# A gated-delta-rule block on one core: where the inverse's read-back waits, and where the merge steps stand among the projections

## The reference

```python
q = short_conv(hidden_states @ Wq, conv_wq).reshape(b, t, NUM_HEADS, HEAD_K)
k = short_conv(hidden_states @ Wk, conv_wk).reshape(b, t, NUM_HEADS, HEAD_K)
v = short_conv(hidden_states @ Wv, conv_wv).reshape(b, t, NUM_HEADS, HEAD_V)
beta = jax.nn.sigmoid(hidden_states @ Wb)
g = -jnp.exp(A_log) * jax.nn.softplus(hidden_states @ Wa + dt_bias)
o = gated_delta_rule(q, k, v, g, beta)
gate = (hidden_states @ Wg).reshape(b, t, NUM_HEADS, HEAD_V)
...
def _step(S, xs):
    qt, kt, vt, gt, bt = xs
    S = S * jnp.exp(gt)[..., None, None]
    pred = jnp.einsum('bhk,bhkv->bhv', kt, S)
    delta = (vt - pred) * bt[..., None]
    S = S + jnp.einsum('bhk,bhv->bhkv', kt, delta)
    return (S, jnp.einsum('bhk,bhkv->bhv', qt, S))
```

## Time and profile before

| | us |
|---|---|
| median of 3 runs | 1102.63 (1102.19 to 1105.66) |
| the profiled execution, its own time | 1100.91 |
| its span, first to last instruction | 1099.1 |
| TensorE busy, matmuls | 1044.1 (95%) |
| VectorE busy | 627.4 (57%) |
| ScalarE busy | 377.8 (34%) |
| GpSimd busy | 212.1 (19%) |

### The profile page before, as it was taken

How to read it: one execution, slowest core, us unless ns; L and a number is a source line. 1 busy time by engine, 2 the same in 40 slices (tenths; PEclk the granted TensorE clock), 3 DMA queues, 4 the chain that set the end, 5 groups by cost and what they waited for, 6 DMA issues and landing times.

```text
span 1099.1 us, 18622 instructions
## 1 busy us (share of the span) xinstructions
PE 1044.1 (95%) x7356; PEld 843.5 (77%) x7356; DVE 627.4 (57%) x986; ACT 377.8 (34%) x691; POOL 212.1 (19%) x166
## 2 busy tenths in 40 slices
PE   3899999999888999999989999999999999999998
PEld 2686667777677888888777787888888888888886
DVE  3778354999884677787766333333333433434356
ACT  3567465354445333333455112121121212122110
POOL 0332100011014545544331000000000000004191
PEclk8899999999899999999999999999999999999999
DMA  6503336736629465666622000010010100001223
GB/s 199 181 30 115 71 65 164 220 97 185 104 60 225 94 144 131 160 163 143 209 74 77 1 1 30 29 34 25 1 58 1 58 1 30 29 1 67 77 77 115
DMA packets 153399, 97.35 MB, mean 89 GB/s; under 512 B 93536, under 2 KB 130656, under 8 KB 153184
## 3 DMA queue, kind: packets, MB, share of 16 engines
q1 hardware_dynamic: 153312, 96.16, 32.0%
HBM read 64.67 MB, written 31.46 MB: 87 GB/s over the span
## 4 chain that ended last, share of the span: by engine, by line
PE 76%; DVE 12%; issue 4%; ACT 3%; DMA 2%; SPq 2%; POOL 0%; DVEq 0%; ACTq 0%
PE ps L1206 72%; DVE t L1795 5%; DVE t L1887 3%; ACT t L1523 3%; PE ps L1214 3%; DVE t L1800 1%; PE ps L1406 1%; DMA t<-in_x 1%; SPq L1086 1%; DMA t<-scrA 1%; SPq L1143 1%; DVE t L1875 1%; DMA t<-scrU 0%; DVE t L1805 0%; DVE t L1987 0%
## 5 line engine op out<-in xcount | busy, mean ns | idle before, releaser
L1206 PE MATMUL ps<-t,t 128*128 128x512 f32 (+6 forms) x6488 | 990.3, 337 | 37.2 <-DMA t<-in_wmod 8.6
L1206 PEld LDWEIGHTS ps<-t,t 128*128 128x128 f32 (+4 forms) x6488 | 785.3, 166 | 218.5 <-issue 38.8
L1795 DVE TENSOR_TENSOR t<-ps,t 128x512 f32<-128x512 f32 (+4 forms) x306 | 208.2, 700 | 257.4 <-PE ps L1206 242.9
L1523 ACT ACTIVATE t<-t 128x512 fp32r<-128x512 f32 (+7 forms) x342 | 190.8, 579 | 327.3 <-DVE t L1795 202.3
L1795 DVE TENSOR_TENSOR t<-t,t 128x512 fp32r<-128x512 f32 (+16 forms) x209 | 164.9, 794 | 116.2 <-ACT t L1523 104.4
L1523 ACT ACTIVATE t<-ps 128x512 f32<-128x512 f32 (+5 forms) x202 | 108.9, 551 | 313.7 <-PE ps L1206 304.9
L2265 POOL TENSOR_TENSOR t<-t,t 128x512 f32<-128x512 f32 x16 | 22.2, 1390 | 375.2 <-DVE t L1795 373.1
L1887 DVE SCALAR_TENSOR_TENSOR t<-ps,t,t 128x511 f32<-128x511 f32 (+2 forms) x108 | 80.3, 747 | 9.0 <-ACT t L1523 6.2
L1214 PE MATMUL ps<-t,t 128*128 128x128 f32 (+1 forms) x388 | 56.8, 280 | 12.2 <-DVE t L1800 9.8
L1214 PEld LDWEIGHTS ps<-t,t 128*128 128x128 f32 (+1 forms) x388 | 43.5, 143 | 25.7 <-DVE t L1800 14.5
L1523 ACT ACTIVATE t<-ps,t 128x512 f32<-128x512 f32 (+2 forms) x96 | 56.9, 621 | 17.8 <-PE ps L1214 9.1
(11 more groups left out here) (49 smaller groups left out, 232.4 us busy)
## 6 DMA issues: line engine op xcount, KB each, us to landing
scrU<-t SPq DMA_DIRECT2D x60, 256.0 KB, 3.0
t<-in_wf SPq DMA_DIRECT2D x16, 768.0 KB, 4.1
t<-scrU SPq DMA_DIRECT2D x32, 288.0 KB, 4.8
t<-in_wmod SPq DMA_DIRECT2D x6, 1024.0 KB, 6.8
t<-scrU SPq DMA_DIRECT2D x32, 192.0 KB, 3.5
t<-in_W SPq DMA_DIRECT2D x19, 256.0 KB, 2.9
t<-in_x SPq DMA_DIRECT2D x16, 256.0 KB, 4.3
t<-in_x SPq DMA_DIRECT2D x32, 128.0 KB, 2.8
```

Of the source, the lines that this page charges most:

```text
L1206: return e.matmul(o, l, r_, start=start, stop=stop, skip_group_check=True)
L1523: return e.activation(o, i, f, **kw)
L1795: return e.tensor_tensor(o, a, b, op)
```

## The change

Three edits. (1) The stores of the inverse signal three semaphores, `d_pp0` to `d_pp2`, in place of one. `inv2_back` of slice s waits only for the stores that hold its blocks, 96 s to 96 s + 95; `clear_p` on GpSimd still waits for all three. (2) The pauses behind the read-backs are six in place of three. (3) While the merge runs (`merging`: inverse made, lane 0 running, before tile 14), a projection is emitted in two halves, k = 0, 1 and k = 2, 3; one step of lane 0 stands between them.

```diff
-    def project(h, b, wn):
+    def project(h, b, wn, ks=(0, 1, 2, 3)):
         i = pr["n"] % 4
         pr["n"] += 1
-        step("proj", h=h, b=b, bank=i, wn=wn, free=bank_free.get(i))
+        step("proj", h=h, b=b, bank=i, wn=wn, free=bank_free.get(i), ks=ks)
         return i, tick("proj")
...
-        for _ in range(3):
+        for _ in range(6):
             yield
         made["inverse"] = 1
...
+            merging = n < 14 and made["inverse"] and running[0]
+            ks = (0, 1) if merging else (0, 1, 2, 3)
             if b < 3:
-                ahead.append(project(nxt, b + 1, wn))
+                ahead.append(project(nxt, b + 1, wn, ks))
...
-                ahead.append(project(nxt, 0, wn))
+                ahead.append(project(nxt, 0, wn, ks))
+            second = {**plan[-1], "ks": (2, 3)} if merging else None
...
+            if merging:
+                side(0, 1)
+                plan.append(second)
             for l in (2, 3, 0, 1):
                 side(l)
...
-                    e.dma_start(blocks[128 * i:128 * i + 128], Pp[:, i, :, :]).then_inc(sem("d_pp"), 16)
+                    e.dma_start(blocks[128 * i:128 * i + 128], Pp[:, i, :, :]).then_inc(sem(f"d_pp{i}"), 16)
             elif kind == "inv2_back":
                 s = st["s"]
-                e.wait_ge(sem("d_pp"), 48)
+                for i in (96 * s // 128, (96 * s + 95) // 128):
+                    e.wait_ge(sem(f"d_pp{i}"), 16)
                 e.wait_ge(*at_least(st["cleared"]))
...
-                for k in range(4):
+                for k in st["ks"]:
                     e.wait_ge(sem("p_lo"), 4 * b + k + 1)
                     t = mm3(bank(st["bank"]), WH[h][:, k, :], WL[h][:, k, :], Hhi[:, b, k, :], Hlo[:, b, k, :],
                             k == 0, k == 3)
-                t.then_inc(sem("proj"), 1)
+                if k == 3:
+                    t.then_inc(sem("proj"), 1)
...
                 elif s == 2:
-                    e.wait_ge(sem("d_pp"), 48)
+                    for i in range(3):
+                        e.wait_ge(sem(f"d_pp{i}"), 16)
```

## The result

The changed kernel is slower: 1105.82 us median (1101.51 to 1109.58, 18 runs) against 1101.95 for the kernel before on the same chips, a ratio of 1.0032 (95% interval 1.0023 to 1.0041). The forecast was 1103.6, +1.0 us on its baseline; the measured difference is about +3.5. The time lies inside the forecast's range, but that range took in both rivals and is 10 us wide; the sum's own ends were -1.2 and +3.4, and the difference lies just above the upper one. It comes out at the slower rival's +3.7, not at the likeliest case. One run of e6_after_free took 1493.32 us at a granted clock of 0.66 and stands in no ratio; every other run named here is a fast one.

The account below looks back on a forecast made before the run. TensorE holds 76% of the chain, but VectorE bounds the merging stage. Taps end 2.6 us earlier, yet the first unit's later load lands the last store 1.0 us later: 1102.63 + 1.0 = 1103.6, range 1097.2 to 1107.0.

Parts of the forecast that it names:

- the sum's own ends: Last tap ending at 320.0 or 323.4, with 7.5 or 8.7 us for the final transfers: -1.2 and +3.4 us.
- slower rival: TensorE's low clock lasts until 293.5 or longer (1.0 more) and falls again later (1.7 more): +3.7, 1106.3; chance 0.27.
- Own stores: At the inverse's read-backs: waiting only for their own stores takes off 0.2 us, at most 0.24.
- The start two slots on, and no wait at the first product: Merge starts in slot (7,0) instead of (6,2); TensorE's 3.62 us wait for the read-back goes.
- ScalarE's wait: In slot (7,0), ScalarE stands from 277.9 to 285.3 for a store queued behind 16 read-backs; TensorE idles 7.1 us.
- VectorE as the bound of the stage: Merging stage: VectorE needs 32.4 us from 288.1, plus 1.5 for low clock; taps end at 322.0, 2.6 us gained.
- a sign against itself: VectorE holes between 291 and 322 would mean the merging stage's bound changed and the last tap's forecast end is off.
- The split's credit of 0.35: Merge steps inside projections bring products before VectorE asks, taking 0.35 of at most 0.85 us off the merging stage.
- The give-back: Behind the last tap: seven merge products remain, delaying unit 0's load to 334.0 and the last store to 341.7; +1.0 us.
- second low stretch in the tail: Slower rival's part: the clock falls again between (8,3) and (14,2), where TensorE is the bound; 1.7 us more.
- faster rival: ScalarE doesn't stand at the merge's start; last store lands at 335.4: -5.3 us, 1097.3; chance 0.20.
- The idle rule: At TensorE's first merge product: removing the wait (3.6) and half the low stretch (3.4) would gain 7.0 us.

Follow-up runs that it names:

- e6_after_free: Changed kernel, but the loads of the first two units no longer wait for the end of the merge; 1102.68 us, ratio 0.9997 to the kernel before.
- e1_store: Kernel before with only the first edit, each read-back waiting for its own store; 1102.66 us, ratio 1.0002 to the kernel before.
- e4_spread: Changed kernel with the read-backs issued one slice a slot, stores of tile 6 between them; 1100.17 us, ratio 0.9977 to the kernel before.
- the second execution: Second profiled execution of the changed kernel, itself unchanged; it took 1107.64 us.
- the first execution: First profiled execution of the changed kernel, the slowest of its 18 runs; it took 1109.58 us.
- e7_fill: Changed kernel with 29 unused matmuls ahead of the first B product, to keep TensorE busy; 1106.67 us, ratio 1.0035 to the kernel before.
- e3_split: Kernel before with only the third edit, a merge step in the middle of each projection; 1101.92 us, ratio 0.9995 to the kernel before.
- e2_late: Kernel before with only the second edit, six pauses instead of three, projections whole; 1104.54 us, ratio 1.0026 to the kernel before.
- e5_spread_free: e4_spread, with the loads of the first two units no longer waiting for the merge's end; 1096.35 us, ratio 0.9941 to the kernel before.
- e10_tail: e5_spread_free with the projections of tile 14 split too; 1095.74 us, ratio 0.995 to the kernel before.

## Why the prediction was right, and where its size was off

**Own stores.** Forecast 0.2 us, at most 0.24; 0.12 measured, no difference in time (e1_store). Right.

**The start two slots on, and no wait at the first product.** Right: the chain has no wait for the landing of a read-back, and A(0) ran at 278.

**ScalarE's wait.** Forecast until 285.3, 7.4 us long, with TensorE idle for 7.1: 7.42 and 7.61 us, 6.58 and 6.80 measured. e4_spread removes it by moving nothing but the read-backs' place in SP's queue. This cause is shown.

**VectorE as the bound of the stage.** T, the end of the last tap, was put at 322.0, 51.7 us behind the first read-back of the forecast (270.55 less 0.2); the second execution has 51.7, the first 55.2. The forecast lets VectorE run on from 288.1 and allows 1.5 us for TensorE's low clock. The chain shows another course: behind the stall TensorE is the bound for 15.05 us in the first execution and for 11.28 in the second, then VectorE, and from 322.88 on, 3.8 us ahead of T, TensorE again. In the first execution VectorE has the holes that the forecast named as a sign against itself, 2.57 us ahead of 296.30 (for TensorE) and 2.21 ahead of 303.69 (for ScalarE). With e7_fill, at full clock, the stretch is 50.6, so the low clock costs 1.1 where it is short and 4.6 where it is long. That 51.7 was met to the tenth is partly luck: it holds for the short low stretch alone, and the kernel before and e1_store differ by 2.6 here. The split's credit of 0.35 can't be told from nothing (e3_split).

**The give-back.** The mechanism was right (e6_after_free), and here the sum is short, in two terms. *From the last tap to the load of unit 0* the forecast was 12.0; it is 13.0 in both executions of the changed kernel, in e4 and in e7. The term that was mis-sized is TensorE's place at T: the forecast has A(12), and so projection (14,0) ahead of it, done at T - 0.25. In the first trace GpSimd's fill, which that projection releases, starts 0.52 behind T (326.65), and ScalarE's eviction of A(12) 1.00 behind it:

```profile
327.17 1.38 POOL L2210 MEMSET t<- 128x1536 f32 x1 [52.77 <-PE ps L1213]
...
327.65 0.67 ACT L1531 ACTIVATE t<-ps 32x192 f32<-32x192 f32 x2 [2.97 <-PE ps L1213]
```

In e2_late, whose projections are whole, the fill starts at 321.62, 0.49 ahead of its T (322.11), and the load 12.3 behind T. So the forecast counted the split as a gain for VectorE alone; the half of (14,0) that it puts behind a merge step is 0.7 of the missing 1.0, as far as two traces can tell. *From there to the landing of the last store* it was 7.7; to the load of Wo, 0.1 later, 9.3 and 8.5 were measured, 9.6 and 9.8 in e7 and e4. The term that was mis-sized is the rate: 1.66 MB at the 266 GB/s of one window, plus one us. The landing of the last store behind three other transfers took 4.82 and 4.40 us where the row of before had 3.09, and 5.40 and 5.58 in e7 and e4; the 8.7 that I had set as the upper end is passed in three of the four traces. In the second execution projection (14,3) ended 16.7 us behind T, where 13.7 was forecast, with 3.4 us at half rate from 335.5 on. As SP's queue was busy until 339.58 anyway, this held up the last store by 0.36 only.

Put together for the second execution: T as forecast, 1.0 and 1.6 more behind it, against a forecast of +1.0: 3.6, with 3.7 seen over the stage (73.95 against 70.21) and about +3.5 in the ratio. For the first execution the same sum gives +6.6 over the stage, more than the ratio, so the agreement rests on the choice of the trace.

**The rivals.** The slower one has the right time (+3.7) for a reason that isn't the main one. Its second low stretch in the tail is there in the second trace:

```profile
334.00:338.00 4.00, 3.89 (x34) 3.19 (x35) 1.39 (x4) 0.06 (x1) 0.00 (x0) 0.70 0.33 74
338.00:342.00 4.00, 3.81 (x63) 3.14 (x62) 0.20 (x1) 2.66 (x4) 1.93 (x3) 0.88 1.19 265
```

but in the first trace the clock is 1.00 there and the tail is nearly as long (21.6 and 22.3 us from the last tap to Wo), and e7_fill, with the clock at 1.00 through both stretches, is as slow. Its first part, a low clock beyond 293.5, is there in the first execution and not in the second. So e2_late and e6_after_free put the loss on the later start and the waiting loads, but how much of it the clock carries in a usual run is open. The faster rival (-5.3, no wait of ScalarE) is what e4_spread builds; it came to 0.23% (2.5 us) under the kernel before, since the give-back stands, and to 0.59% (6.5) with the loads freed (e5). The chance of 0.26 for slower and 0.52 for no change was the wrong way round for a loss of 0.32%, right at the edge between them.

**The idle rule.** By the rule of the Trainium skill (TensorE: Matmul & The Clock Gate, "Why this matters for your kernels"), to leave TensorE no idle gap between bursts of matmuls, the change would gain 7.0 us by the prediction's estimate, the wait and the half of its low stretch. The trace agrees that a low stretch follows a stall (0.66 and 0.50 behind 6.58 us of idleness), and e7_fill that filling matmuls keep the clock up. But the wait was only moved, from 3.62 us to 6.58, and the kernel with the clock kept up isn't faster (1.0035 against 1.0032).

## What to carry to other kernels

Before you let a producer start later so that nobody waits for its data, look at what else is queued behind that data on its DMA queue: a burst of 16 small read-backs (11 us in the queue) held up one unrelated store, and through the buffer that the store frees it stopped ScalarE, TensorE and VectorE in turn. Issue such a burst in pieces between the stores of the running work. And when work is moved past the end of a stage, find the loads of the next stage that wait for it by a semaphore: freeing them from a wait that no memory asked for was worth as much here as the whole loss.

## What the runs showed of the hardware

A stall of 6.6 to 6.8 us at the same place of the same program was followed by 6.8 us at half rate in one execution and by 17.1 in two others. The clock fell behind 1.94 us of idleness in e4_spread and e10_tail as well, while in e5_spread_free, with 1.96 us of idleness at the same place, it stayed at 1.00. Between the two executions of the changed kernel the longer low stretch goes with 3.5 us more up to the last tap, as much as the change did. So a profile that stands at the edge of its kernel's runs needs a second one before its low stretches are costed, and the second has to be compared with its own runs as well.

A store of 256 KB took 3.09 us to land in the kernel before, 4.40 to 5.58 when it was issued right behind three other transfers, and at most 2.4 on a quiet queue (e5_spread_free).
